# One attention and mixture-of-experts layer on one core: the order of the projection stage's stores and loads, and two instructions' places in it

## The reference, cut to what matters

```python
x = L0_attn_x                                    # (4, 1024, 256) float32
xn = _layernorm(x, axis=-1)
x = x + _L0_attn_ref(xn, Wq, Wk, Wv, Wo, bo) + _L0_ffn_ref(xn, ...)

# _L0_attn_ref: 16 heads of 16, causal, with a bias that grows with the distance
q = (x @ Wq).reshape(b, s, H, D).transpose(0, 2, 1, 3)
k = (x @ Wk).reshape(b, s, H, D).transpose(0, 2, 1, 3)
v = (x @ Wv).reshape(b, s, H, D).transpose(0, 2, 1, 3)
scores = jnp.einsum('bhqd,bhkd->bhqk', q, k)
...
w = jax.nn.softmax(scores, axis=-1)
ctx = jnp.einsum('bhqk,bhkd->bqhd', w, v).reshape(b, s, e)
return ctx @ Wo + bo

# _L0_ffn_ref: 8 experts, each token goes to two of them
router_input = x * jax.lax.rsqrt(var + 1e-06) * root_size * router_scale
logits = jnp.einsum('gsd,de->gse', router_input, router_logits)
...
```

## Time and profile before

| | |
|---|---|
| time, median of 3 runs | 815.77 us (812.65 to 816.36) |
| the profiled execution: its time, its span | 815.55 us, 813.8 us |
| busy: PE, DVE, ACT, POOL | 94%, 67%, 57%, 53% |
| the projection stage | from the start to about 123 us |

### The profile page before, as it was taken

The page is one execution under the profiler, slowest core; times in us unless marked ns, Lnnn a source line. Parts: engine busy times, 40 slices in busy tenths (PEclk is TensorE's granted clock), DMA queues, the critical chain, the costliest instruction groups (busy, mean ns, idle before and its releaser), DMA issues.

```text
span 813.8 us, 17685 instructions
## 1 busy us (share of the span) xinstructions
PE 766.9 (94%) x6172; PEld 468.4 (58%) x6172; DVE 546.2 (67%) x1419; ACT 466.9 (57%) x984; POOL 433.7 (53%) x561
## 2 busy tenths in 40 slices
PE   8999999999999999999999999879899899998997
PEld 6555554444444434444444444328889789888976
DVE  5458879999999888888888888303344334433348
ACT  3564567777777677777777777774333333333310
POOL 7665542231324545655475453264686667666676
PEclk9999999999999999999999999999999999999999
DMA  8895562513233134243442350113533333322777
GB/s 202 250 296 175 171 190 57 157 34 91 81 93 99 40 96 131 61 103 106 107 98 66 95 158 16 36 41 88 155 104 111 111 105 111 104 84 83 235 247 240
DMA packets 74912, 98.20 MB, mean 121 GB/s; under 512 B 16588, under 2 KB 54092, under 8 KB 74764
## 3 DMA queue, kind: packets, MB, share of 16 engines
q1 hardware_dynamic: 65960, 78.34, 34.2%
q0 software_dynamic: 8864, 18.72, 7.4%
HBM read 63.53 MB, written 30.75 MB: 116 GB/s over the span
## 4 chain that ended last, share of the span: by engine, by line
PE 50%; POOL 13%; issue 12%; ACT 4%; DVE 3%; DMA 2%; another core or an unknown queue 1%; DVEq 0%; POOLq 0%; ACTq 0%
PE banks L1154 17%; PE banks L754 16%; PE banks L746 13%; POOL expert_rows L1243 7%; POOL stacks L593 5%; ACT probs L1092 4%; PE banks L1339 3%; DVE stacks L1438 2%; PE banks L1348 1%; DMA stacks<-xn_rows,places 1%; DVE junk L708 1%; PE banks L1269 0%; DMA w_gu<-expert_rows 0%; DMA expert_rows<-stacks,places 0%
## 5 line engine op out<-in xcount | busy, mean ns | idle before, releaser
L708 DVE CUSTOM_DVE_ANT_0 junk<-banks,mask 128x128 bf16<-128x128 f32 (+7 forms) x512 | 359.6, 753 | 55.7 <-issue 50.6
L1092 ACT ACTIVATE probs<-banks 128x512 f32<-128x512 f32 x576 | 310.7, 606 | 102.7 <-PE banks L754 98.4
L754 PE MATMUL banks<-stacks 105*128 105x512 bf16 (+3 forms) x768 | 199.4, 329 | 10.1 <-issue 5.4
L746 PE MATMUL banks<-stacks 102*128 102x512 bf16 (+3 forms) x768 | 172.6, 326 | 2.2 <-DVE maxima L708 2.0
L885 POOL TENSOR_SCALAR_AFFINE_SELECT probs<-probs 128x512 f32<-128x512 f32 x128 | 79.9, 643 | 103.3 <-ACT probs L1092 99.5
L1321 DVE TENSOR_TENSOR probs<-banks,probs 128x256 f32<-128x256 f32 x71 | 30.1, 423 | 150.6 <-ACT probs L1285 125.0
L754 PEld LDWEIGHTS banks<-stacks 105*128 105x128 bf16 x768 | 65.6, 97 | 103.5 <-ACT probs L1092 40.5
L1154 PE MATMUL banks<-probs,ctxT 128*17 128x256 f32 (+2 forms) x1920 | 114.4, 360 | 2.0 <-DVE banks L1073 1.1
L1243 POOL DMA_INDIRECT expert_rows<-stacks,places x71 | 79.9, 1126 | 62.4 <-ACT stacks L1290 48.1
L746 PEld LDWEIGHTS banks<-stacks 102*128 102x128 bf16 x768 | 69.1, 98 | 72.2 <-DVE maxima L708 17.5
L1285 ACT ACTIVATE probs<-banks 128x256 f32<-128x256 f32 x71 | 27.3, 385 | 109.7 <-PE banks L1339 66.4
(11 more groups left out here) (129 smaller groups left out, 781.2 us busy)
## 6 DMA issues: line engine op xcount, KB each, us to landing
stacks<-qk_parts SPq DMA_DIRECT2D x192, 128.0 KB, 3.1
qk_parts<-ctxT SPq DMA_DIRECT2D x32, 384.0 KB, 3.3
xn_rows<-probs SPq DMA_DIRECT2D x8, 512.0 KB, 5.1
ctxT<-inverse_sums SPq DMA_DIRECT2D x8, 512.0 KB
w_gu<-in_w_gu SPq DMA_DIRECT2D x8, 512.0 KB
stacks<-in_x SPq DMA_DIRECT2D x16, 256.0 KB
ctxT<-expert_rows SPq DMA_DIRECT2D x16, 256.0 KB, 3.6
w_gu<-expert_rows SPq DMA_DIRECT2D x16, 256.0 KB, 5.5
```

The source lines that it names most:

```text
L708: last = dve.tensor_tensor_reduce(junk[:, n % RING, c:c + w], mpsum[:, slot, c:c + w], keep["mask"][:, S - w:S], 1.0, 3 * NEG, ALU.add, AL ...
L746: last = pe.matmul(mpsum[:, slot, at + c:at + e], qs[hq][0:R_MAX, h, qt * P:(qt + 1) * P], ks[hq][0:R_MAX, h, c:e], start=True, stop=True)
L754: last = pe.matmul(score_bank(("S", n, h))[:, c:c + w], ks[hq][:, h, kt * P:(kt + 1) * P], qs[hq][:, h, q0:q0 + w], start=True, stop=True)
L1092: act.activation(probs[:, u % PRING, h], score_bank(("S", n, h)), ACT.Exp, scale=SCALE).then_inc(exp_done, 1)
```

## The change

It does four things. SyncE stores a chunk's normalised rows ahead: chunk 0's before the constants, chunk 1's behind chunk 0's parts, and from then on those of chunk c+1 behind the second quarter of chunk c's parts. The load of the rows of x for chunk c+4 moves from the start of chunk c's stores to their end. The constants (`map`, `escale`, and the eight transfers of `c_q` and `c_k`) move from the start to behind chunk 0's parts, chunk 1's rows and chunk 4's load of x. VectorE normalises chunk 1 one quarter earlier, behind the first subtraction ("rest") of chunk 0 and not behind the second. TensorE issues chunk 3's early product at place 7 behind the fourth group of v and not behind the third.

```diff
-        def stores(c, par, load):
+        def store_rows(c, par):
             sp.wait_ge(xn_ready, c + 1)
             sp.dma_start(xn_rows[ds(c, 1)].rearrange("a p t d -> (a p) t d"), xn[:, par]).then_inc(x_stored[par], 16)
-            if load:
-                sp.dma_start(x_in[:, c % XR], x_rows[c + XR]).then_inc(x_loaded[c % XR], 16)
+
+        def stores(c, par, load):
             if c == 2:
...
                              parts[:, q]).then_inc(parts_stored[q], 16)
+                if q == 1 and 0 < c < NC - 1:
+                    store_rows(c + 1, 1 - par)
                 if (c, q) == (NC - 1, 1):
                     ahead["maxima_rows"](sp, 0, 0)
                 if (c, q) in ROWS_AT:
                     load_rows(sp, scratch, heads, 0, *ROWS_AT[c, q])
-
-        sp.wait_ge(unused_set, 3)
-        sp.dma_start(scratch["map"]...)
-        sp.dma_start(keep["escale"][:, :], ...)
-        for q in range(NQ):
-            sp.dma_start(heads["qs"][q][R_ALIBI:R_MAX, :, :], ins["c_q"][q]).then_inc(heads["const_in"], 16)
-            sp.dma_start(heads["ks"][q][R_ALIBI:ROWS, :, :], ins["c_k"]).then_inc(heads["const_in"], 16)
+            if c == 0:
+                store_rows(1, 1)
+            if load:
+                sp.dma_start(x_in[:, c % XR], x_rows[c + XR]).then_inc(x_loaded[c % XR], 16)
+
+        store_rows(0, 0)
         for c in range(NC):
             stores(c, c % 2, c + XR < NC)
+            if c == 0:
+                (the lines taken out above)
...
-                if (c, q) == (0, 2):
+                if (c, q) == (0, 1):
                     normalise(1, 1, 0)
...
-                if nxt and t in (0, 2):
-                    early(c, 6 + t // 2)
+                if nxt and t in (0, 3):
+                    early(c, 6 + t // 3)
```

More of the change, by code:

```diff
@@ L345, in stores @@
                     load_rows(sp, scratch, heads, 0, *ROWS_AT[c, q])
-        sp.wait_ge(unused_set, 3)
-        sp.dma_start(scratch["map"].rearrange("(p s) c -> p (s c)", p=P), unused[:, :, :].rearrange("p s c -> p (s c)")).then_inc(map_stored, 16)
-        sp.dma_start(keep["escale"][:, :], ins["expert_scale"].partition_broadcast(P)).then_inc(map_stored, 16)
-        for q in range(NQ):
-            sp.dma_start(heads["qs"][q][R_ALIBI:R_MAX, :, :], ins["c_q"][q]).then_inc(heads["const_in"], 16)
-            sp.dma_start(heads["ks"][q][R_ALIBI:ROWS, :, :], ins["c_k"]).then_inc(heads["const_in"], 16)
+            if c == 0:
[3 more added lines that the diff above has]
+        store_rows(0, 0)
         for c in range(NC):
             stores(c, c % 2, c + XR < NC)
+            if c == 0:
+                sp.wait_ge(unused_set, 3)
+                sp.dma_start(scratch["map"].rearrange("(p s) c -> p (s c)", p=P), unused[:, :, :].rearrange("p s c -> p (s c)")).then_inc(map_stored, 16)
+                sp.dma_start(keep["escale"][:, :], ins["expert_scale"].partition_broadcast(P)).then_inc(map_stored, 16)
+                for q in range(NQ):
+                    sp.dma_start(heads["qs"][q][R_ALIBI:R_MAX, :, :], ins["c_q"][q]).then_inc(heads["const_in"], 16)
+                    sp.dma_start(heads["ks"][q][R_ALIBI:ROWS, :, :], ins["c_k"]).then_inc(heads["const_in"], 16)
     def on_gpsimd(pool):
```

## The result

| | before | after |
|---|---|---|
| time, median of 17 runs each | 814.74 us (810.55 to 818.32) | 817.66 us (814.36 to 821.23) |
| the profiled execution: its span | 813.8 us | 815.2 us |

The ratio is 1.0041, with a 95% interval of 1.0025 to 1.0056: 2.0 to 4.6 us slower, so the loss is small but clear of zero, and the ratio itself lies inside the 0.5% that the forecast called "within". The forecast was 819.7, and the sum +4.1.

The account below looks back on a forecast made before the run. The prediction took PE, working in 94% of the span, to bound the kernel. Against the profiled 815.55 us, +3.7 - 0.44 + 0.8 = +4.1 us gave 819.7 us, with an 8-in-10 range of 813.2 to 821.8.

Parts of the forecast that it names:

- Normalise earlier: VectorE's normalise of chunk 1: its instructions take 1.38 us, not 3.05, and PE's wait before the transposes goes; -0.55 us.
- Chunk 1's wait: PE's third group in chunk 1: chunk 0's parts land near 20.1 without constants ahead, ending the wait; -2.05 us.
- The constants moved: SyncE's queue behind chunk 0: the constants hold later transfers as long as now, so chunk 1's first parts land at 40.0.
- The first rival: Constants are slow only beside other traffic, so at the new place nothing waits: 812.5 to 813.5 us; chance 0.13.
- PE in chunk 2: PE's third group in chunk 2 starts at 41.5 and not 38.2, waiting for chunk 1's first parts; +3.2 us.
- The row loads and the fourth group of chunk 3: Chunk 2's row loads start at 44.3, its second parts land at 56.4, PE's fourth group starts at 57.9; +3.7 us in all.
- Place 7: Chunk 3's early product: the fourth group of v fills PE's wait for VectorE's maxima; -0.44 us, bounds 0 and -0.9.
- Rows and x moved: Rows stored earlier and x loaded later cost nothing: rows are needed two chunks later, x over a chunk after issue.
- The clock: PE's clock falls to half behind a wait of over 3 us, costing 0 to 1.7 us in chunk 3; half taken, +0.8.

Follow-up runs that it names:

- norm_alone: The kernel before with only chunk 1's normalise one quarter earlier, behind chunk 0's first subtraction; 820.29 us in one run.
- x_behind_alone: The kernel before with only the load of x moved to the end of a chunk's stores; 813.11 us, ratio 0.9993 to before.
- consts_ahead: The changed kernel with the eight c_q and c_k transfers ahead of chunk 0's rows again; 821.66 us, ratio 0.9913 to before.
- rows_apart: The changed kernel with constants spread among early stores, plus the eight transfers again as a block into unused rows 11 partitions apart; 816.15 us in one run.
- kept_busy: The changed kernel with 20 useless transposes on PE ahead of chunk 2's third group, filling its wait; 827.12 us in one run.
- spread_behind: The changed kernel with constants spread among early stores and a chunk's rows stored behind the row loads sharing their place; 820.68 us, ratio 0.9906 to before.
- ahead_behind: The changed kernel with the eight constants ahead of the first store and rows stored behind the row loads sharing their place; 808.98 us, ratio 0.9928 to before.
- consts_spread: The changed kernel with two constants behind chunk 0's rows and one behind each of the first six stores of parts; 820.11 us, ratio 0.9896 to before.
- after_again: The changed kernel once more, unchanged, on the chip of the second set; 818.09 us, ratio 1.0048 to before.

## Why the prediction was right

- **Normalise earlier, -0.55.** Chunk 1 begins 0.67 earlier, though chunk 0 begins 0.15 later: 0.82. VectorE's four instructions took 1.37. But its worth hangs on the next step: alone it made the stage 2.0 longer, in one trace, 1.7 of it by the clock (norm_alone).
- **Chunk 1's wait, -2.05.** Exact in size: 11.58 us, and no wait. The reason was wrong in part. The step said "What held them up is the constants"; with the constants where they were and x moved behind, the wait is gone too (x_behind_alone, consts_ahead). The constants made the parts late, and the load of x made them too late. The move of x brings this gain without the constants' cost; that the constants' move would bring it as well is an estimate (22.9, above).
- **The constants moved.** The step "at 28.3 + 11.7 = 40.0" met the landing to 0.01, and the four behind it (41.0, 42.3, 43.3, 44.3) landed at 40.96, 42.30, 43.31 and 44.35. That is luck in part: x landed at 29.6 and not at 28.3, and the hold was 10.4 and not 11.7. That the constants are slow without other traffic too is shown by the nine packets in 29.7 to 30.5, and that it hangs on where the rows lie by rows_apart. The estimate of 9.6 us from the port's rate in the Trainium skill (SBUF — State Buffer, "Door 1: The DMA port swizzle") agrees with the trace: the first of their packets starts at 28.9 and the last is over at 38.5. The first rival, 812.5 to 813.5, fell with it.
- **PE in chunk 2, +3.2.** The third group started at 41.46, forecast 41.5, with a wait of 3.15.
- **The row loads and the fourth group of chunk 3, +3.7 in all.** Row loads at 44.43 (forecast 44.3), second parts at 52.77 (52.7), landed at 56.4 (56.4). kept_busy shows that this landing is enough: with chunk 3 begun at 49.5, PE's fourth group waited for it until 57.54. Of the signs forecast here one did not come: ScalarE stood 1.28 and not 3 us in chunk 3, as the clock had made chunk 3 begin 3 us later.
- **Place 7, -0.44.** -0.54 alone.
- **Rows and x moved, nothing.** Wrong by a little: the step looked at who waits for the rows and not at what stands behind their store in SyncE's queue. In chunk 6 these are row loads, which now start 4.04 us before chunk 7 and not 4.57. PE waits 0.35 for them, and chunk 7 is 0.5 longer in all (the distance to before is 3.25 at its start and 3.76 at its end). spread_behind and ahead_behind take it away.
- **The clock, +0.8.** The wrong place and the wrong size: it fell in chunk 2 for 6.8 us, not in chunk 3. It delayed chunk 3 by 3 us, above the step's 1.7, but "in chunk 2 the row loads cover it": the wait of chunk 3 shrank to nearly nothing on PE, and without the fall (kept_busy) chunk 4 begins no earlier than its parts land. So the term was worth nothing.

The sum from the runs: +3.7 - 0.54 + 0.5 = +3.7, and the stage's end in the trace is 3.6 behind. The forecast was 0.4 above this: the clock's 0.8 too much and place 7 a tenth too little gain, against the 0.5 in chunk 7. That two wrong terms nearly cancel is luck; the large one, the constants' hold and the row loads behind it, is not. The time shows +2.9 by the medians and 2.0 to 4.6 by the interval, so it cannot tell 3.7 from 4.1.

## What to carry to other kernels

A transfer off the critical path is to be judged by what it holds in its queue at its new place, and the place before a wait that gathers several landings is the dearest one. When two causes lie on one landing, take each away alone before naming one: here moving the load of x was enough for the gain, and moving the constants in one block gave the change its cost. An edit that starts work earlier ahead of an unchanged landing only lengthens the wait, and a longer wait can take the clock with it.

## What the runs showed of the hardware

- Of the eight transfers' 60 rows the first 15 took 0.3 to 0.7 us a packet in the trace of after, those behind them 0.9 to 1.25, mostly about 1.2, in 28.9 to 38.5. Spread out (consts_spread, at most 15 rows together) 45 of the 60 took 0.31, and the longest 0.99. So a short burst into neighbouring partitions cost next to nothing here, and only the long one held the queue. That first packets are fast says nothing about a rate, which the forecast had against its first rival.
- A transfer into rows 11 partitions apart takes SyncE 0.70 to 0.85 us to issue (rows_apart), into neighbouring ones 0.27 to 0.57, six of eight up to 0.32 (after).
- Waits of PE and the clock behind them: after 3.15 us in chunk 2, 3.82 in after_again, both with the clock at 0.50 for 6.8 us; 2.92 in norm_alone, 0.50 for 3.4 us; 1.77 in before, 2.56 in kept_busy and 2.91 in rows_apart no fall. 2.91 and 2.92 lie on both sides, so the length of the wait alone doesn't decide; what does isn't shown.
